# Joining and scaling the attention context ahead of its output product

## The chip, the cores and the metric

One core of a Trainium2 chip runs the whole program. The metric is the device time of one execution in microseconds; three executions of the kernel before took 811.64, 813.15 and 817.57 us.

## The reference

Four layers run one after another on 1024 rows of 256 numbers: a latent attention, a mixture of 64 experts, a recurrent mixer and a mixture of 8 experts, each added to its input and normalised. The change touches only the first. Cut to what matters:

```
kv = rmsnorm(compressed[:, :64]) @ kv_b.T         # per head: 128 of keys, 128 of values
scores = (q @ k.T) * scaling, masked to the causal half      # 16 heads
probs  = softmax(scores)
out    = concat over heads of (probs @ v)
x      = layernorm(x + out @ o_proj.T)
```

The kernel works in the latent space of 64 numbers: for a head, `context = latent.T @ exp(scores).T` has 64 rows, and the value and the output projections are multiplied once into one 64x256 matrix per head (`wvo`). The softmax's division by the row sum is made last.

## The kernel before

**Groups.** The attention goes through 8 tiles of 128 query rows; tile t looks at (t+1)*128 keys. Four heads form a group, so there are 32 groups, numbered G, four in a tile. Of each head TensorE makes scores in three passes (L1673 to L1675, high and low halves of float32) and adds the causal mask (L1760); VectorE takes the row maximum (L1133); ScalarE makes the exponential and the row sum (L868).

**Blocks.** A group's probabilities are then taken in t+1 blocks of 128 keys. For each block TensorE transposes four 128x128 pieces into one PSUM bank (L1788), ScalarE copies the rounded half out (`copy_hi`, L875), VectorE subtracts it to get the rest (`copy_lo`, L1139), and TensorE adds two products to the context in the bank `misc` (`context`, L1801 and L1803). `latent` holds high and low parts side by side, so the upper 64 and the lower 64 partitions of the context are two terms of one sum.

**Output.** When a group's context is complete, ScalarE copies it to SBUF (`copy_ctx`, L881). One group later TensorE multiplies, head by head, the context of 128 partitions with `wvo`, which holds the same 64 rows twice (`output`, L1810). VectorE scales the product of each head by the reciprocal of its row sum and adds it to the sum so far (`add_head`, L1156); the reciprocals of a group are one instruction on 128x4 numbers (`invert`, L1144).

**Order.** Each engine runs a list written out by hand: `head_slots` goes through four slots i of each G, and in a slot each engine does its part for the scores of a head of group G, for the blocks of group G-1 (at eight places, two in a slot) and for the output of group G-2. In a slot VectorE does in this order: `add_head`, steps of the normalisation and of the routing of the tile before, `copy_lo` of the first place, the row maximum, `copy_lo` of the second place, and in slot 1 `invert`. An engine does not pass an instruction that waits.

**Banks.** Blocks, outputs of heads and the small products of the routing are `tenants`: they take PSUM banks in turn, four of them while scores use short rows (the first 64 heads), then three, and seven for the last group. Before TensorE writes a bank, `take_seat` waits until the tenant before it has been read.

**Start and end.** The SP queue loads the input, the weights and a broadcast row `lnw`, in that order; a stage before the attention makes the queries, `wvo` and the keys. After the attention its last tile is normalised and routed before the experts can start.

The lines that set the order of the three engines in a slot:

```
def pe_slot(G, i, n):
    steps(G, 2 * i)
    for m in heads_at(n):
        scores(m)
    steps(G, 2 * i + 1)
    if 0 <= G - 2 < GROUPS:
        output(QUAD * (G - 2) + i)
```

Of the kernel before, what the change touches and what calls it, by code (L numbers as in the profile page):

```python
# [6 lines left out]
P = 128  # L7
# [7 lines left out]
BANK = 512  # L15
# [10 lines left out]
TWO_OUTS = SHORT - 3 * QUAD  # L26
# [12 lines left out]
def build(nc, x, xT, wq, wq_ropeT, wkv_aT, kv_ln, wkv_b, woT, router0T, gate_up0, down0, w_in, init_state,  # L39
# [5 lines left out]
    with ctx:  # L45
# [51 lines left out]
        wvo = cutA3(HEADS * HID)  # L97
# [14 lines left out]
        rinv = sb("rinv", [P, 3, QUAD])  # L112
        y = sb("y", [P, HID])
        sgd = sb("sgd", [P, 2, BANK])
        ctxT = sgd
# [127 lines left out]
        def out_of(n):  # L243

            return seat_of("out", n)[:, 0:HID]

# [4 lines left out]
        ld_x, ld_xT, ld_kv = (sem(n) for n in ("ld_x", "ld_xT", "ld_kv"))  # L251
# [8 lines left out]
        pT_ps, hi_done, lo_done, ctx_step, ctx_copied, rinv_done, out_ready, out_read = (  # L260
            sem(n) for n in ("pT_ps", "hi_done", "lo_done", "ctx_step", "ctx_copied", "rinv_done", "out_ready",
                             "out_read"))
# [158 lines left out]
        for G in range(GROUPS + 1):  # L421
            for spot in range(8):
                if route_at(G, spot):
                    tenants.append((route_at(G, spot), tile_of(G) - 1))
                tenants += [("block", b) for b in blocks_at(G - 1, spot)]
                if spot % 2 and 0 <= G - 2:
                    tenants.append(("out", QUAD * (G - 2) + spot // 2))
        tenants += [("out", QUAD * (GROUPS - 1) + i) for i in range(QUAD)]
# [6 lines left out]
        LENT = pT + [acc, half[3]] + half[0:3]  # L435
        long_rows = seat("out", TWO_OUTS)
# [52 lines left out]

        def head_slots(body):  # L490
# [5 lines left out]

        @block.sync
# [334 lines left out]
        def _(act):  # L832
            act.wait_ge(kv_ready, 1)
# [63 lines left out]
            def act_slot(G, i, n):  # L897
# [5 lines left out]
                if i == QUAD - 1 and 0 <= G - 1 < GROUPS:  # L903
                    copy_ctx(G - 1)
# [173 lines left out]
        def _(dve):  # L1078
            dve.wait_ge(ld_xT, 16)
            dve.tensor_copy(xT_hi[:], xT_in[:]).then_inc(x_split, 1)  # L1080
            dve.wait_ge(x_split, 1)
            dve.tensor_tensor(xT_lo[:], xT_in[:], xT_hi[:].bitcast(f32), ALU.subtract).then_inc(x_split, 1)
# [11 lines left out]
            def wvo_copy(m):  # L1094

                hold(dve, wvo_ps, 2 * m + 2)
                dve.tensor_copy(wvo[:, bass.ds(2 * m * HID, 2 * HID)], misc[:]).then_inc(wvo_done, 1)
# [22 lines left out]
            wvo_copy(0)  # L1120
# [4 lines left out]
            wvo_copy(1)  # L1125
            with dve.Fori(2, PAIRS) as j:
                split_weff(2 * j, 0, j)
                split_weff(2 * j + 1, 1, j)
                wvo_copy(j)
# [16 lines left out]
            def add_head(n):  # L1146

                t, h = divmod(n, HEADS)
                s, k = stat_of(n)
                dve.wait_ge(out_ready, n + 1)  # L1150
                if h == 0:
                    dve.wait_ge(ld_x, 32)
                    dve.wait_ge(rinv_done, n // QUAD + 1)
                else:
                    dve.wait_ge(out_read, n)
                dve.scalar_tensor_tensor(x1[:, t, :], out_of(n), rinv[:, s, k:k + 1], x1[:, t, :] if h else x_in[:, t, :],  # L1156
                                         ALU.mult, ALU.add).then_inc(out_read, 1)
# [18 lines left out]
            def attention_variance(t):  # L1176
                dve.wait_ge(out_read, (t + 1) * HEADS)
# [69 lines left out]
            def dve_slot(G, i, n):  # L1247
# [20 lines left out]
                go_on()  # L1268
                for b in blocks_at(G - 1, 2 * i):
# [17 lines left out]
            add_head(TILES * HEADS - 1)  # L1287
# [381 lines left out]
        def _(pe):  # L1669
# [15 lines left out]
            pe.wait_ge(ld_xT, 16)  # L1685
            pe.wait_ge(ld_kv, 16)
            for t in range(TILES):
                for c in range(HC):
# [33 lines left out]
            pe.wait_ge(x_split, 2)  # L1722
# [23 lines left out]
            def scores(n):  # L1746
# [4 lines left out]
                if n == SHORT + 1:  # L1751
                    await_read(*max((tenants[j] for j in range(long_rows) if seats[j] == 3), key=tenants.index))
# [17 lines left out]
            def await_read(before_it, k):  # L1770
                if before_it == "out":
                    pe.wait_ge(out_read, k + 1)
# [19 lines left out]
            def context(G, k):  # L1792
# [3 lines left out]
                if k == 0:  # L1796
                    if G:
                        pe.wait_ge(ctx_copied, G)
# [6 lines left out]
            def output(n):  # L1805
                G, i = divmod(n, QUAD)
                pe.wait_ge(ctx_copied, G + 1)
                take_seat("out", n)
                h = n % HEADS
                pe.matmul(out_of(n), ctxT[:, G % 2, i * P:(i + 1) * P], wvo[:, h * HID:(h + 1) * HID],  # L1810
# [356 lines left out]
```

## Time and profile before

| | us |
|---|---|
| median of 3 runs | 813.15 |
| the profiled execution | 812.66 |
| its span, first to last instruction | 810.9 |
| TensorE busy (matmuls) | 768.1 |
| VectorE busy | 555.0 |
| ScalarE busy | 397.7 |
| attention: first to last copy of a context (L881) | 80.6 to 404.2 |

### The profile page before, as it was taken

The numbers are of one execution on the slowest core, as the hardware profiler recorded it, in microseconds if no ns is written. First come the engines' busy times: TensorE is split into PE (matmuls) and PEld (weight loads), VectorE is DVE, ScalarE is ACT, GpSimd is POOL, SyncE is SP. The second block draws the span as 40 slices with busy tenths as digits, with TensorE's granted clock in tenths as the row PEclk, the third lists the DMA queues.
The fourth block names the chain that finished last, engine by engine and source line by source line (L and its number), as shares of the span: only waits on it lengthen the run. The fifth ranks groups of instructions, "written<-read, shape, count | busy, mean of one in ns | idle before, by whom it ended". The sixth has DMA issues, their size and how long they took to land.

```text
span 810.9 us, 16066 instructions
## 1 busy us (share of the span) xinstructions
PE 768.1 (95%) x4619; PEld 652.6 (80%) x4619; DVE 555.0 (68%) x1401; ACT 397.7 (49%) x899; POOL 309.7 (38%) x408
## 2 busy tenths in 40 slices
PE   8999989999999999999989999889999999999997
PEld 7887867777778788777778999788887888888885
DVE  5323778787868778777746666468858388888546
ACT  1234656656656566566514444313343266666431
POOL 2004446443433333322345665625444233333341
PEclk9999999999999999999999999999999999999999
DMA  7349971000000000009238899777651234555331
GB/s 215 100 112 340 404 296 46 29 29 28 24 26 23 21 22 22 21 15 327 87 104 296 282 363 362 267 267 278 242 184 72 72 94 153 152 152 155 111 111 52
DMA packets 61282, 120.75 MB, mean 149 GB/s; under 512 B 18016, under 2 KB 30816, under 8 KB 61088
## 3 DMA queue, kind: packets, MB, share of 16 engines
q1 hardware_dynamic: 52864, 96.59, 35.9%
q0 software_dynamic: 8352, 23.34, 8.0%
q8 instruction: 33, 0.54, 0.3%
q14 instruction: 33, 0.27, 0.1%
HBM read 76.13 MB, written 43.78 MB: 148 GB/s over the span
## 4 chain that ended last, share of the span: by engine, by line
PE 71%; DVE 10%; issue 8%; DMA 4%; POOL 3%; ACT 3%; SPq 1%; DVEq 0%; ACTq 0%; POOLq 0%
PE scores L1673 9%; PE scores L1675 9%; PE scores L1674 9%; PE scores L1897 6%; PE acc_ps L2093 5%; PE misc_ps L1803 4%; PE misc_ps L1801 4%; PE probsT_ps L1788 3%; PE probsT_ps L1810 3%; PE scores L1907 3%; PE probsT_ps L2027 3%; PE acc_ps L1788 3%; DVE xT_lo L1139 2%; DVE neg_max L1133 2%; PE probsT_ps L1886 1%
## 5 line engine op out<-in xcount | busy, mean ns | idle before, releaser
L868 ACT ACTIVATE area<-scores,neg_max 128x128 f32<-128x128 f32 (+7 forms) x128 | 94.9, 742 | 86.3 <-DVE neg_max L1133 85.9
L1133 DVE TENSOR_REDUCE neg_max<-scores 128x1 f32<-128x128 f32 (+7 forms) x128 | 95.8, 749 | 21.8 <-PE scores L1760 21.7
L711 POOL DMA_INDIRECT xe_d<-x_rows,send_i x64 | 64.0, 1001 | 55.3 <-ACT x_rows L892 38.5
L751 POOL DMA_INDIRECT ye_d<-area,home_i x64 | 61.4, 959 | 39.1 <-DVE home_i L1340 18.4
L699 POOL CAST weff_hi<-area 128x256 fp32r<-128x256 f32 x42 | 16.6, 395 | 135.1 <-PE scores L1760 87.5
L1673 PE MATMUL scores<-kT_hi,weff_hi 128*128 128x512 f32 (+3 forms) x172 | 66.6, 387 | 0.9 <-ACT area L845 0.4
L1897 PE MATMUL scores<-area 128*96 128x128 f32 x512 | 66.4, 273 | 0.4 <-issue 0.4
L1675 PE MATMUL scores<-kT_hi,weff_lo 128*128 128x512 f32 (+3 forms) x172 | 61.5, 358 | 0.0
L1674 PE MATMUL scores<-kT_lo,weff_hi 128*128 128x512 f32 (+3 forms) x172 | 61.4, 357 | 0.0
L1803 PE MATMUL misc_ps<-xT_lo,xT_hi 128*128 128x512 f32 x144 | 58.3, 405 | 1.9 <-DVE xT_lo L1139 1.8
L1897 PEld LDWEIGHTS scores<-area 128*96 128x96 f32 x512 | 59.2, 163 | 0.7 <-issue 0.6
L1788 PE MATMUL probsT_ps<-ident,area 128*128 128x128 f32 x320 | 48.1, 274 | 5.3 <-DVE xT_lo L1139 5.1
L1810 PE MATMUL probsT_ps<-area,sgd 128*128 128x256 f32 x162 | 49.6, 388 | 0.7 <-DVE xT_lo L1139 0.4
L1139 DVE TENSOR_TENSOR xT_lo<-probsT_ps,xT_hi 128x512 fp32r<-128x512 f32 x53 | 36.1, 685 | 18.3 <-ACT xT_hi L875 18.2
L1801 PE MATMUL misc_ps<-xT_hi 128*128 128x512 f32 x96 | 47.4, 494 | 0.1
L801 POOL DMA_INDIRECT area<-x_d,home x23 | 22.3, 970 | 63.7 <-ACT sgd L1013 45.3
L1673 PE MATMUL scores<-xT_hi,weff_hi 128*128 128x512 f32 x110 | 46.1, 419 | 0.0
L1788 PEld LDWEIGHTS probsT_ps<-ident,area 128*128 128x128 f32 x320 | 35.8, 142 | 11.1 <-issue 8.1
L2093 PE MATMUL acc_ps<-area 128*128 128x256 f32 x184 | 43.5, 379 | 0.8 <-DVE area L1557 0.8
L1675 PE MATMUL scores<-xT_hi,weff_lo 128*128 128x512 f32 x110 | 43.4, 394 | 0.0
L706 POOL TENSOR_TENSOR rstd<-mv,minus_half 128x1 f32<-128x1 f32 x28 | 17.0, 607 | 68.7 <-DVE mv L1165 68.7
L1674 PE MATMUL scores<-xT_lo,weff_hi 128*128 128x512 f32 x110 | 43.0, 391 | 0.0
(308 smaller groups left out, 2069.8 us busy)
## 6 DMA issues: line engine op xcount, KB each, us to landing
area<-w SPq DMA_DIRECT2D x23, 512.0 KB, 4.2
area<-gate_up SPq DMA_DIRECT2D x24, 384.0 KB, 5.1
xe_d<-area SPq DMA_DIRECT2D x8, 1088.0 KB, 11.4
ye_d<-area SPq DMA_DIRECT2D x8, 1024.0 KB, 16.9
area<-w SPq DMA_DIRECT2D x8, 1024.0 KB, 7.6
area<-ye_d SPq DMA_DIRECT2D x15, 512.0 KB, 5.0
area<-xe_d SPq DMA_DIRECT2D x28, 272.0 KB, 6.1
area<-down SPq DMA_DIRECT2D x24, 192.0 KB, 6.6
```

Source lines behind the costliest of these rows:

```text
L711: pool.indirect_dma_start(xe_d, bass.IndirectOffsetOnAxis(send_i[:, t, k:k + 1], 0), x1_rows[:, t, :], None).then_inc(sent[k % 2] if t < T ...
L868: act.activation(row_of(n)[:, 0:L], score_bank(n)[:, 0:L], ACT.Exp, bias=neg_max[:, n % 4:n % 4 + 1], accum_out=rsum[:, s, k:k + 1]).then_ ...
L1133: dve.tensor_reduce(neg_max[:, n % 4:n % 4 + 1], score_bank(n)[:, 0:(n // HEADS + 1) * P], AX.X, ALU.max, negate=True).then_inc(max_ready, 1)
L1673: pe.matmul(out_ap, lh, rh, start=start, stop=False)
L1674: pe.matmul(out_ap, lh, rl, start=False, stop=False)
L1675: return pe.matmul(out_ap, ll, rh, start=False, stop=stop)
L1788: last = pe.transpose(seat_of("block", b)[:, i * P:(i + 1) * P], row_of(QUAD * G + i)[:, k * P:(k + 1) * P], ident[:])
L1801: pe.matmul(ctx_ps[:], latent[:, k, :], pT_hi[b % 3], start=k == 0, stop=False)
L1803: pe.matmul(ctx_ps[:], latent[:, k, :], pT_lo[b % 3], start=False, stop=k == tile_of(G)).then_inc(ctx_step, 1)
L1810: pe.matmul(out_of(n), ctxT[:, G % 2, i * P:(i + 1) * P], wvo[:, h * HID:(h + 1) * HID], start=True, stop=True).then_inc(out_ready, 1)
L1897: last = pe.matmul(half[b][0:I0, part * P:(part + 1) * P], weights_of(e)[0][:, c, part * I0:(part + 1) * I0], xeT[:, b, c, :], start=c == ...
L2093: last = pe.matmul(acc[:, 0:HID], hdT[:, u, c * P:(c + 1) * P], w2_b[:, u, c, :], start=c == 0, stop=c == I1 // P - 1)
```

## The change

- ScalarE no longer copies the context as it is. It copies the upper 64 partitions of the group's first two heads to the lower 64, and the lower 64 of the other two to the upper (`cross_ctx`); VectorE adds to each the half that lay there (`join_ctx`). The result is 128x256: two heads of 64 rows on top of each other.
- The reciprocals are written out on 128x256 numbers, each one 64 times, read from a broadcast (`invert`); TensorE transposes them (`spread_scales`) and VectorE multiplies the joined context with them (`scale_ctx`).
- TensorE multiplies two heads in one contraction over 128 partitions (`output`), and sums all eight products of a tile in PSUM, in the bank `acc`. VectorE adds the input once a tile (`add_out`).
- `acc` leaves the banks in turn: three, then two, and six for the last group. A group's tenants are its blocks and one for the transposed scales.
- `wvo` holds two heads on top of each other, so its copies take 64 partitions each.
- At the start the input arrives in two halves, the second from ScalarE's queue, and so does `lnw`; VectorE splits the halves one by one.

```diff
-                banks_now = 4 if k < long_rows else 3 if k < tail else 7
+                banks_now = 3 if k < long_rows else 2 if k < tail else 6
...
-            sp.dma_start(xT_in[:], xT.rearrange("(c p) t -> p c t", p=P)).then_inc(ld_xT, 16)
+            sp.dma_start(xT_in[:, :, 0:BANK], xT_v[:, :, 0:BANK]).then_inc(ld_xT[0], 16)
...
-            sp.dma_start(lnw[:], bass.AP(kv_ln.tensor, 0, [[0, P], [1, RANK]])).then_inc(ld_head[1], 16)
...
+            act.dma_start(xT_in[:, :, BANK:], xT_v[:, :, BANK:]).then_inc(ld_xT[1], 16)
+            act.dma_start(lnw[:], bass.AP(kv_ln.tensor, 0, [[0, P], [1, RANK]])).then_inc(ld_head[1], 16)
...
-            def copy_ctx(G):
+            def cross_ctx(G):
                 act.wait_ge(ctx_step, blocks_to(G + 1))
                 if G >= 2:
-                    act.wait_ge(out_ready, QUAD * (G - 1))
-                act.copy(ctxT[:, G % 2, :], ctx_ps[:]).then_inc(ctx_copied, 1)
+                    act.wait_ge(ctx_used, scaled_at(G - 2))
+                act.copy(ctx_joined[LOW, G % 2, :], ctx_ps[HIGH, 0:HID]).then_inc(ctx_crossed, 1)
+                act.copy(ctx_joined[HIGH, G % 2, :], ctx_ps[LOW, HID:]).then_inc(ctx_crossed, 1)
...
             def invert(G):
                 dve.wait_ge(probs_ready, QUAD * (G + 1))
-                dve.reciprocal(rinv[:, G % 3, :], rsum[:, G % 3, :]).then_inc(rinv_done, 1)
...
+                wide = [P, 2, 2, RANK]
+                dve.reciprocal(rinv[:, G % 3].rearrange("p j (b r) -> p j b r", b=2),
+                               rsum[:, G % 3, :].rearrange("p (b j) -> p j b", b=2).unsqueeze(3).broadcast_to(wide)
+                               ).then_inc(rinv_done, 1)
+
+            def join_ctx(G):
+
+                dve.wait_ge(ctx_crossed, 2 * G + 2)
+                for rows, part in ((LOW, slice(0, HID)), (HIGH, slice(HID, 2 * HID))):
+                    dve.tensor_tensor(ctx_joined[rows, G % 2, :], ctx_ps[rows, part], ctx_joined[rows, G % 2, :],
+                                      ALU.add).then_inc(ctx_used, 1)
+
+            def scale_ctx(G):
+
+                dve.wait_ge(scales_and_out, scales_at(G))
+                dve.wait_ge(ctx_used, joined_at(G))
+                dve.tensor_tensor(ctxT[:, G % 2, :], seat_of("scales", G)[:, 0:HID], ctx_joined[:, G % 2, :],
+                                  ALU.mult).then_inc(ctx_used, 1)
+
+            def add_out(t):
+
+                dve.wait_ge(scales_and_out, out_at(SETS * t + SETS - 1))
+                dve.wait_ge(ld_x, 32)
+                dve.tensor_tensor(x1[:, t, :], out_ps, x_in[:, t, :], ALU.add).then_inc(ctx_used, 1)
...
-                behind = n - 1 - 2 * QUAD
-                if 0 <= behind < TILES * HEADS:
-                    add_head(behind)
+                behind = 0 <= G - 2
+                if behind and i == 0:
+                    join_ctx(G - 2)
+                if behind and i == QUAD - 1 and (G - 2) % SETS == SETS - 1:
+                    add_out(tile_of(G - 2))
...
                 go_on()
+                if behind and i == 0:
+                    scale_ctx(G - 2)
...
+            def spread_scales(G):
+
+                pe.wait_ge(rinv_done, G + 1)
+                take_seat("scales", G)
+                for j in range(2):
+                    last = pe.transpose(seat_of("scales", G)[:, j * P:(j + 1) * P],
+                                        rinv[:, G % 3, j, :], ident[:])
+                last.then_inc(scales_and_out, 1)
+
+            def output(G):
+
+                pe.wait_ge(ctx_used, scaled_at(G))
+                if G >= SETS and G % SETS == 0:
+                    pe.wait_ge(ctx_used, added_at(tile_of(G) - 1))
+                for j in range(2):
+                    m = G % SETS * 2 + j
+                    last = pe.matmul(out_ps, ctxT[:, G % 2, j * P:(j + 1) * P],
+                                     wvo[:, m * HID:(m + 1) * HID], start=m == 0, stop=m == PAIRS - 1)
+                last.then_inc(scales_and_out, 1)
...
-                if 0 <= G - 2 < GROUPS:
-                    output(QUAD * (G - 2) + i)
+                if i == 2 and 0 <= G - 2:
+                    output(G - 2)
+                if i == 3 and 0 <= G - 1 < GROUPS:
+                    spread_scales(G - 1)
```

## Rows read from the trace of the kernel before

**Rows 1.** The page, part 1: busy us, share of the span, instructions of each engine.

```profile
PE 768.1 (95%) x4619; PEld 652.6 (80%) x4619; DVE 555.0 (68%) x1401; ACT 397.7 (49%) x899; POOL 309.7 (38%) x408
```

**Rows 2.** Busy time in windows of the attention: stretch, length, engines, clock, DMA.

```profile
78.00:122.00 44.00, 40.64 (x257) 33.52 (x257) 33.51 (x98) 25.66 (x84) 20.75 (x36) 1.00 0.90 353
122.00:192.00 70.00, 67.16 (x386) 51.94 (x385) 56.47 (x137) 42.70 (x105) 34.39 (x49) 1.00 0.09 33
192.00:402.00 210.00, 200.04 (x1185) 164.49 (x1184) 162.08 (x316) 128.80 (x251) 67.32 (x93) 1.00 0.16 56
128.50:135.90 7.40, 6.83 (x43) 5.42 (x40) 6.71 (x16) 4.87 (x15) 4.91 (x7) 1.00 0.10 39
```

**Rows 3.** Chain of work that ended last, two pieces: start us, length us, what.

```profile
301.11 0.44 PE acc_ps L1788 x4
...
302.02 0.43 PE probsT_ps L1810 x2
```

**Rows 4.** Groups of VectorE's instructions by line, attention: busy us, mean ns, idle before.

```profile
L1156 DVE SCALAR_TENSOR_TENSOR x_rows<-probsT_ps,rinv,x_rows 128x256 f32<-128x256 f32 x76 | 35.8, 470 | 0.8 <-PE probsT_ps L1810 0.7
...
L1144 DVE RECIPROCAL rinv<-rsum 128x4 f32<-128x4 f32 x32 | 5.3, 166 | 0.0
```

**Rows 5.** Groups by line and shape, whole span: VectorE, 256 numbers wide; ScalarE's copies.

```profile
L1561 DVE TENSOR_TENSOR weff_lo<-misc_ps,weff_hi 128x256 fp32r<-128x256 f32 x23 | 9.8, 424 | 17.2 <-ACT weff_hi L1019 17.2
...
L881 ACT COPY sgd<-misc_ps 128x512 f32<-128x512 f32 x32 | 18.7, 583 | 12.9 <-PE misc_ps L1803 12.9
...
L1031 ACT COPY area<-acc_ps 128x256 f32<-128x256 f32 x23 | 8.6, 372 | 22.6 <-PE acc_ps L2093 22.6
```

**Rows 6.** The same view: other reciprocals, and another VectorE operation at like widths.

```profile
L1165 DVE TENSOR_SCALAR mv<-mv 128x1 f32<-128x1 f32 x28 | 4.3, 153 | 1.0
...
L1633 DVE RECIPROCAL rstd<-root 128x1 f32<-128x1 f32 x4 | 0.6, 142 | 0.0
...
L1299 DVE RECIPROCAL wsum<-wsum 128x8 f32<-128x8 f32 x1 | 0.2, 203 | 0.0
...
L1103 DVE TENSOR_SCALAR ms<-ms 128x8 f32<-128x8 f32 x1 | 0.2, 173 | 0.0
```

**Rows 7.** Waits in the attention: who for whom, us in total, times, longest.

```profile
DVE xT_lo L1139 <- ACT xT_hi L875: 36.9, 45, 1.6
...
PE probsT_ps L1788 <- DVE xT_lo L1139: 5.1, 6, 1.6
PE acc_ps L1788 <- DVE xT_lo L1139: 5.1, 6, 1.7
```

**Rows 8.** Timeline, VectorE around three reciprocals: start, length, instruction, idle before it.

```profile
120.44 0.17 DVE L1144 RECIPROCAL rinv<-rsum 128x4 f32<-128x4 f32 x1
...
120.90 0.55 DVE L1133 TENSOR_REDUCE neg_max<-scores 128x1 f32<-128x384 f32 x1
...
199.41 0.17 DVE L1144 RECIPROCAL rinv<-rsum 128x4 f32<-128x4 f32 x1
...
200.40 0.69 DVE L1139 TENSOR_TENSOR xT_lo<-acc_ps,xT_lo 128x512 fp32r<-128x512 f32 x1 [0.46 <-ACT xT_lo L875]
...
400.42 0.17 DVE L1144 RECIPROCAL rinv<-rsum 128x4 f32<-128x4 f32 x1
...
401.15 0.69 DVE L1139 TENSOR_TENSOR xT_lo<-acc_ps,xT_hi 128x512 fp32r<-128x512 f32 x1 [0.19 <-ACT xT_hi L875]
```

**Rows 9.** Timeline at the attention's end: last copy of a context, last sum.

```profile
404.23 0.59 ACT L881 COPY sgd<-misc_ps 128x512 f32<-128x512 f32 x1 [1.39 <-PE misc_ps L1803]
...
407.37 0.48 DVE L1156 SCALAR_TENSOR_TENSOR x_rows<-scores,rinv,x_rows 128x256 f32<-128x256 f32 x1
```

**Rows 10.** Timeline of the first 11 us: SP's slow issue, warming matmuls, first product.

```profile
2.30 3.77 SPq L502 DMA_DIRECT2D lnw<-kv_ln  x1
...
2.36 4.63 PE L1681 MATMUL misc_ps<-ident 128*128 128x128 f32 x20 [2.36 <-POOL ident_bf L664]
...
6.78 4.02 PE L1689 MATMUL scores<-area 128*128 128x128 f32 x32
```

More of the change, by code:

```diff
@@ L96, in build @@
         weff_lo = sb("weff_lo", [P, 2, HC, P], f32r)
-        wvo = cutA3(HEADS * HID)
+        wvo = cutA3(PAIRS * HID)
         qT = area1
@@ L111, in build @@
         rsum = sb("rsum", [P, 3, QUAD])
-        rinv = sb("rinv", [P, 3, QUAD])
+        rinv = cutA3(3, 2, P)
         y = sb("y", [P, HID])
         sgd = sb("sgd", [P, 2, BANK])
-        ctxT = sgd
+        ctx_joined, ctxT = (sgd[:, :, part * HID:(part + 1) * HID] for part in range(2))
+        LOW, HIGH = slice(0, RANK), slice(RANK, P)
         stats = sb("stats", [P, 6])
@@ L241, in build @@
         ctx_ps = misc
-        def out_of(n):
-            return seat_of("out", n)[:, 0:HID]
         half = [banks[u][:, b * BANK:(b + 1) * BANK] for u in range(2) for b in range(2)]
-        ld_x, ld_xT, ld_kv = (sem(n) for n in ("ld_x", "ld_xT", "ld_kv"))
+        ld_x, ld_kv = (sem(n) for n in ("ld_x", "ld_kv"))
+        ld_xT = [sem(f"ld_xT{b}") for b in range(2)]
         ld_head = [sem(f"ld_head{u}") for u in range(2)]
@@ L420, in build @@
         tenants = []
-        for G in range(GROUPS + 1):
+        for G in range(GROUPS + 2):
             for spot in range(8):
@@ L425, in build @@
                 tenants += [("block", b) for b in blocks_at(G - 1, spot)]
-                if spot % 2 and 0 <= G - 2:
-                    tenants.append(("out", QUAD * (G - 2) + spot // 2))
-        tenants += [("out", QUAD * (GROUPS - 1) + i) for i in range(QUAD)]
+                if spot == 7 and 0 <= G - 1 < GROUPS:
+                    tenants.append(("scales", G - 1))
         tenants += [(what, TILES - 1) for what in route_places.values()]
@@ L433, in seat @@
             return tenants.index((what, n))
-        LENT = pT + [acc, half[3]] + half[0:3]
-        long_rows = seat("out", TWO_OUTS)
+        LENT = pT + [half[3]] + half[0:3]
+        out_ps = acc[:, 0:HID]
+        long_rows = seat("scales", SHORT // QUAD - 3) + 1
         tail = seat("block", blocks_to(GROUPS - 1))
@@ L488, in stat_of, with scales_at, out_at, joined_at @@
             return n // QUAD % 3, n % QUAD
+        def scales_at(G):
+            return 2 * G + 1
+        def out_at(G):
+            return 2 * G + 2
+        def joined_at(G):
+            return 3 * G + G // SETS + 2
+        def scaled_at(G):
+            return 3 * G + G // SETS + 3
+        def added_at(t):
+            return (3 * SETS + 1) * (t + 1)
         def head_slots(body):
@@ L1078, in _ @@
         def _(dve):
[L1079 to L1082, printed above, removed]
+            x_halves = [slice(0, BANK), slice(BANK, T)]
+            for b, part in enumerate(x_halves):
+                dve.wait_ge(ld_xT[b], 16)
+                dve.tensor_copy(xT_hi[:, :, part], xT_in[:, :, part]).then_inc(x_split, 1)
+            for b, part in enumerate(x_halves):
+                dve.wait_ge(x_split, b + 1)
+                dve.tensor_tensor(xT_lo[:, :, part], xT_in[:, :, part], xT_hi[:, :, part].bitcast(f32),
+                                  ALU.subtract).then_inc(x_split, 1)
             def split_weff(h, u, i):
@@ L1124, in _ @@
             split_keys(1)
[L1125 to L1129, printed above, removed]
+            wvo_copy(1, 0, HIGH)
+            with dve.Fori(1, SETS) as s:
+                for b, rows in enumerate((LOW, HIGH)):
+                    split_weff(4 * s + 2 * b, 0, 2 * s + b)
+                    split_weff(4 * s + 2 * b + 1, 1, 2 * s + b)
+                    wvo_copy(2 * s + b, s, rows)
             def row_max(n):
@@ L1751, in scores @@
                 if n == SHORT + 1:
-                    await_read(*max((tenants[j] for j in range(long_rows) if seats[j] == 3), key=tenants.index))
+                    await_read(*max((tenants[j] for j in range(long_rows) if seats[j] == 2), key=tenants.index))
                 q = q_his[n // 2 % 3][:, n % 2, :], q_los[n // 2 % 3][:, n % 2, :]
@@ L1770, in await_read @@
             def await_read(before_it, k):
[L1771 to L1772 removed]
+                if before_it == "scales":
+                    pe.wait_ge(ctx_used, scaled_at(k))
                 elif before_it == "block":
@@ L1803, in context @@
                 pe.matmul(ctx_ps[:], latent[:, k, :], pT_lo[b % 3], start=False, stop=k == tile_of(G)).then_inc(ctx_step, 1)
[L1805 to L1810, printed above, removed]
-                          start=True, stop=True).then_inc(out_ready, 1)
+            def spread_scales(G):
[14 more added lines that the diff above has]
+                last.then_inc(scales_and_out, 1)
             def transpose_x1(t):
```

37 lines of the change are left out of this document (13 added, 24 removed).

## The prediction

> **What bounds the kernel now.** I read the page's busy times first: TensorE is busy for 95% of the span, VectorE for 68% [rows 1]. That is an average over the layers, so the windows of the attention come next, the only stage that the change reworks. TensorE is busy 92 to 96% in each of them, VectorE 76%, 81% and 77% (33.51 of 44.00, 56.47 of 70.00, 162.08 of 210.00 us), ScalarE about 60% [rows 2]. Read by that alone, TensorE is the bound and each matmul taken away is time won.
>
> The waits speak against it. VectorE's `copy_lo` waits 36.9 us for the rounded halves of one buffer from ScalarE, and TensorE's transposes wait 10.2 us, in twelve places, for `copy_lo` to free a bank [rows 7]. The three engines run in a ring: scores, maximum, exponential, rounded copy, `copy_lo`, next transposes. Where the ring is tight, a microsecond on VectorE stops TensorE. So the question for each part is what VectorE's list looks like afterwards.
>
> The Trainium skill (Perfetto Trace Analysis, Identifying the Most-Contended Engine) says that matmul busy time does not tell how near TensorE is to its limit, and that the share of weight loads tells it better. The trace agrees in direction: weight loads cover 33.52 of 44.00, 51.94 of 70.00 and 164.49 of 210.00 us [rows 2]. By busy matmuls all of the work removed below would come back as time; by weight loads a part of it was never the limit.
>
> **TensorE's part.** Before, a head's output product holds TensorE for 0.43 us [rows 3], a group's four for 1.72. After, a group has two products, 0.86, and two transposes of scales, half of the 0.44 us of four [rows 3]: 1.08 us. That is 0.64 us less in each of 32 groups, 20.5 us in all, if TensorE were never kept waiting.
>
> **ScalarE's part.** One copy of 0.583 us becomes two of 256 columns at 0.372 [rows 5]: 0.16 us more per group on an engine with 40% idle. I cost it at nothing; the exponential behind it has the row maximum to wait for anyway. Copies that cross the partitions are not in the trace; the bounds are 0, if each takes half of the one before, and 0.58 us more, if each takes all of its 0.583.
>
> **VectorE's part, the price that decides.** Removed per group: four `add_head` at 0.470 and a reciprocal at 0.166 [rows 4], 2.05 us. Added: two joins, one scaling and a quarter of `add_out`, 3.25 instructions at the 0.424 us of a 256-wide operation that reads PSUM [rows 5], 1.38 us; and a reciprocal of 128x256.
>
> No row has a reciprocal that wide. Its lower bound is any other operation of that width, 0.424 us. But reciprocals grow steeply: 142 ns for one number a partition, 166 for four, 203 for eight, while another operation goes from 153 to 173 [rows 4 to 6]. The slope is (203-142)/7 = 8.7 ns a number, three times the other's 2.9. Carried to 256, 142 + 255 x 8.7 gives 2.36 us; with the flattest pair (8.0) 2.18, with the steepest (9.25) 2.50. I take 2.3, since the rows of the same operation are nearer than those of other ones.
>
> The Trainium skill (VectorE: DVE Perf Modes, First, the fixed hardware budget) says that the reciprocal is an iterative division with a repeat count of 8. By that rule the sum is the one below; by the 256-wide row VectorE would have a little less to do than before, and the second rival would hold.
>
> So VectorE gets 1.38 + 2.3 - 2.05 = 1.63 us more per group.
>
> **Where that falls.** The wide reciprocal stands where the small one stood, at the end of slot 1, and ahead of the next `copy_lo` or maximum.
>
> Tiles 0 to 3: in tile 1 the next maximum follows the reciprocal within 0.3 us, after one `add_head` and with no idle time [rows 8]; there VectorE is nearly the bound. In the densest stretch it reached 6.71 of 7.40 us, 90% [rows 2], so I let it be at most that busy. The first window needs (33.51 + 8 x 1.63)/0.90 = 51.7 us instead of 44, 7.7 more; the second (56.47 + 13.0)/0.90 = 77.2 instead of 70, 7.2 more.
>
> Tiles 4 to 7: sixteen groups. Here `copy_lo` comes next and starts 0.56 to 1.43 us after the reciprocal's end, 1.08 in the mean (the first, 0.82, and the last, 0.56, are shown [rows 8]): room left by the vanished `add_head` and the wait for ScalarE. The reciprocal grows by 2.13 us, so `copy_lo` comes 1.05 us later, and behind it the bank that TensorE's next transposes need, or the block that the next product needs. In sixteen groups that is 16.8 us. The 0.64 us that TensorE saves lies ahead of these waits and mostly lengthens them. The joins and the scaling, 1.27 us in slot 0, lie beside ScalarE's exponential and rounded copy, which `copy_lo` waits for; I cost them at nothing; without that cover they would be 0.8 us per group more than the `add_head` they replace.
>
> **Banks.** With two in turn a block waits for the one two before it, whose `copy_lo` its context product awaits right after. The second block of each group instead takes the bank of the scales and so waits for `scale_ctx`. In tiles 6 and 7 only 0.22 + 0.44 us of TensorE's work lie between the last context product and that block, against 2 x 0.372 + 3 x 0.424 = 2.02 us of crossing, joining and scaling: a wait of some 1.4 us in 8 groups, 11 us. I take nothing, as ScalarE cannot copy this block before the last head's exponential and the first block are through; 11 stays as the upper bound.
>
> **Start and end.** SP's issue of `lnw` took 3.77 us and leaves its queue. But the warming matmuls ran from 2.36 to 6.99, and the first product with the input, on which all that follows waits, started among their last at 6.78 [rows 10]: 0, between 1 us won by earlier weights and 1 lost to two queues loading at once. The half-partition copies of `wvo` do as many columns as before: 0. At the end 3.62 us lay between the last copy's start and the last sum's end [rows 9]; afterwards it is 0.74 + 1.27 + 0.86 + 0.42 = 3.3 and two more hand-overs, 0.3 more.
>
> **Sum.** 7.7 + 7.2 + 16.8 + 0.3 = 32 us on the profiled 812.66, which lies 0.49 under the median: **845 us**.
>
> **Rivals.**
> 1. TensorE is the bound all through, and the reciprocal is no longer than other operations: 20.5 us come back, 792 us. For it speaks the 95%; against it the waits and the slope of three reciprocals. It decides wherever VectorE keeps idle time behind the reciprocal. Chance 0.08.
> 2. The reciprocal is short, but the wait for the scales' bank in tiles 6 and 7 (11 us) and the ring eat most of what TensorE saves: 812.66 - 20.5 + 11 = 803 to 813, say 810. Chance 0.08.
> 3. Nothing of VectorE's extra work is hidden: 32 x 1.63 = 52 us, with the bank's 11 on top 864 to 876. Against it speak 77% of VectorE busy in tiles 4 to 7. Chance 0.06.
>
> That leaves 0.78 for the forecast. Its own range runs from 819, with VectorE 95% busy in the early tiles (4.9 + 3.2 - the start's 1) and little lost later, to 864. To hold 8 in 10 I go from 817 to 867.
>
> A measurement of this kernel can tell about 1%, 8 us, from no change. Faster than 805: rival 1 and a small part of rival 2, 0.09. Within: the rest of rival 2 and the forecast's low edge, 0.10. Slower than 821: 0.81.
>
> **What would show it.** Right: 32 reciprocals of 128x256 at 2.2 to 2.5 us each; VectorE's busy time in the attention up by some 50 us while TensorE's falls; TensorE's waits for `copy_lo` after slot 1 grown by about 1 us a group; the attention some 30 us longer, all else unchanged. Wrong: a wide reciprocal near 0.4 us would bring down the whole forecast; a long one with the attention not longer would mean that VectorE's idle time lies where I saw none.

## The result, and the profile after

The change made the kernel slower: 868.76 us in the median (867.21 to 869.99) against 813.28 for the kernel before beside it, a ratio of 1.068 with a 95% interval of 1.064 to 1.073. The prediction had the direction; 845 us was 24 us too low, and the time lies just over the end of the range, 867.

The page of the changed kernel, busy time by engine; it answers to [rows 1]:

```profile
PE 773.3 (89%) x4555; PEld 652.4 (75%) x4555; DVE 596.4 (69%) x1379; ACT 405.3 (47%) x931; POOL 309.3 (36%) x408
```

TensorE went from 95% to 89%, VectorE from 68% to 69%, and the span grew by 57 us. So the added time is mostly waiting. VectorE has 41 us more to do, and TensorE is busy for 5 us more, although the change was to take 20.5 us off it: it ran at a lower clock, as the windows show.

The windows of the attention, laid over the same tiles as [rows 2] (tiles 0 and 1, 2 and 3, 4 to 7): start and end, length, busy time of PE, PEld, DVE, ACT and POOL, TensorE's granted clock, DMA share, GB/s:

```profile
80.00:136.00 56.00, 40.63 (x241) 32.37 (x242) 42.96 (x92) 27.79 (x90) 20.99 (x35) 0.97 0.69 271
136.00:218.00 82.00, 65.67 (x372) 49.76 (x371) 66.53 (x131) 44.37 (x114) 33.31 (x49) 0.98 0.08 28
218.00:460.00 242.00, 205.50 (x1150) 166.27 (x1149) 184.34 (x306) 132.86 (x266) 67.85 (x94) 0.94 0.14 49
```

The three stretches grew by 12, 12 and 32 us. All of the loss is in the attention. The granted clock, 1.00 in each stretch before, is 0.94 to 0.98. Of the prediction's signs of being right, VectorE's 50 us more came as 42 (252.06 to 293.83 over the three stretches); TensorE's fall did not come (307.84 to 311.80).

VectorE's new groups in the attention: busy time and mean, then idle before. The first answers to the 128x4 reciprocal of [rows 4], the others to the 256-wide operation of [rows 5]:

```profile
L1167 DVE RECIPROCAL area<-rsum 128x256 f32<-128x256 f32 x32 | 55.8, 1743 | 0.0
L1175 DVE TENSOR_TENSOR sgd<-misc_ps,sgd 64x256 f32<-64x256 f32 x62 | 26.2, 422 | 14.4 <-ACT sgd L897 13.0
L1182 DVE TENSOR_TENSOR sgd<-probsT_ps,sgd 128x256 f32<-128x256 f32 x27 | 11.4, 421 | 2.1 <-DVE sgd L1175 0.5
```

The reciprocal takes 1.74 us, not 2.3. Joins and scaling took the 0.42 us forecast for them.

TensorE's waits in the attention; they answer to [rows 7] (in total, times, longest):

```profile
PE probsT_ps L1824 <- DVE sgd L1182: 32.1, 21, 2.6
PE probsT_ps L1824 <- DVE xT_lo L1161: 10.0, 11, 1.9
PE misc_ps L1839 <- DVE xT_lo L1161: 6.9, 15, 1.4
```

The transposes' wait for `copy_lo` did not grow (10.2 us before). That of the context products did; before, it was

```profile
PE misc_ps L1803 <- DVE xT_lo L1139: 1.8, 5, 0.7
```

A new wait stands above both: transposes that wait for `scale_ctx` to free the bank of the scales. With two more of them that write to a bank of another name (3.4 us) it comes 23 times, 35.5 us in all. This is the wait that the prediction saw and took nothing for. The timeline of TensorE shows one of them (start, length, instruction, idle time before it):

```profile
414.06 0.60 PE L1824 MATMUL probsT_ps<-ident,area 128*128 128x128 f32 x4
417.29 0.63 PE L1824 MATMUL probsT_ps<-ident,area 128*128 128x128 f32 x4 [2.63 <-DVE sgd L1182]
417.67 0.68 PE L1708 MATMUL scores<-kT_hi,weff_hi 128*128 128x512 f32 x1
```

And the stretch right behind it, in the windows (columns as above):

```profile
417.84:421.24 3.40, 3.40 (x13) 2.50 (x13) 1.27 (x2) 0.60 (x1) 2.66 (x3) 0.51 1.03 334
```

TensorE idles for 2.63 us and then runs at 0.51, the 1.2 GHz level: this wait is paid twice. The attention has 11 stretches of 3.41 us at that level, 37.5 us in all; the profiled execution of the kernel before had none there.

### The profile page after: what moved, and what is told of

It reads as the page before. It is cut to its first block, busy times and chain, and to the rows that moved or that the text cites. A ratio compares the mean times of both kernels' runs of the same rounds, so it can differ in the third digit from the quotient of the medians.

```text
span 868.2 us, 15777 instructions
## 1 busy us (share of the span) xinstructions
PE 773.3 (89%) x4555; PEld 652.4 (75%) x4555; DVE 596.4 (69%) x1379; ACT 405.3 (47%) x931; POOL 309.3 (36%) x408
## 4 chain that ended last, share of the span: by engine, by line
PE 61%; DVE 19%; issue 10%; ACT 5%; POOL 3%; DMA 2%; DVEq 0%; SPq 0%; ACTq 0%; POOLq 0%
PE scores L1708 8%; PE scores L1710 8%; PE scores L1709 8%; PE scores L1947 6%; PE probsT_ps L1824 5%; PE acc_ps L2143 5%; DVE xT_lo L1161 4%; DVE area L1167 3%; PE scores L1957 3%; DVE neg_max L1155 3%; PE misc_ps L1839 3%; PE misc_ps L1837 3%; DVE sgd L1175 2%; PE probsT_ps L2077 2%; PE acc_ps L1857 2%
## 5 line engine op out<-in xcount | busy, mean ns | idle before, releaser
L1824 PE MATMUL probsT_ps<-ident,area 128*128 128x128 f32 x508 | 83.0, 291 | 42.5 <-DVE sgd L1182 32.1
L1155 DVE TENSOR_REDUCE neg_max<-scores 128x1 f32<-128x128 f32 (+7 forms) x128 | 94.7, 747 | 31.7 <-PE scores L1796 31.6
L1824 PEld LDWEIGHTS probsT_ps<-ident,area 128*128 128x128 f32 x508 | 60.8, 151 | 53.5 <-issue 30.5
L712 POOL CAST weff_hi<-area 128x256 fp32r<-128x256 f32 x42 | 16.6, 394 | 158.4 <-PE scores L1796 110.7
L1161 DVE TENSOR_TENSOR xT_lo<-probsT_ps,xT_hi 128x512 fp32r<-128x512 f32 x85 | 57.8, 682 | 18.4 <-ACT xT_hi L890 17.9
L890 ACT ACTIVATE xT_hi<-probsT_ps 128x512 fp32r<-128x512 f32 x85 | 50.1, 594 | 37.9 <-PE probsT_ps L1824 37.9
L1839 PE MATMUL misc_ps<-xT_lo,xT_hi 128*128 128x512 f32 x144 | 60.1, 417 | 6.9 <-DVE xT_lo L1161 6.9
L1167 DVE RECIPROCAL area<-rsum 128x256 f32<-128x256 f32 x32 | 55.8, 1743 | 0.0
```

Source lines behind the costliest of these rows:

```text
L1155: dve.tensor_reduce(neg_max[:, n % 4:n % 4 + 1], score_bank(n)[:, 0:(n // HEADS + 1) * P], AX.X, ALU.max, negate=True).then_inc(max_ready, 1)
L1161: dve.tensor_tensor(pT_lo[b % 3], seat_of("block", b)[:], pT_hi[b % 3].bitcast(f32), ALU.subtract).then_inc(lo_done, 1)
L1167: dve.reciprocal(rinv[:, G % 3].rearrange("p j (b r) -> p j b r", b=2), rsum[:, G % 3, :].rearrange("p (b j) -> p j b", b=2).unsqueeze(3). ...
L1824: last = pe.transpose(seat_of("block", b)[:, i * P:(i + 1) * P], row_of(QUAD * G + i)[:, k * P:(k + 1) * P], ident[:])
L1839: pe.matmul(ctx_ps[:], latent[:, k, :], pT_lo[b % 3], start=False, stop=k == tile_of(G)).then_inc(ctx_step, 1)
```

## The experiments

**Theories.** They have the letters of the expectations. A: the one wait for the scales' bank costs the time. B: the wide reciprocal on VectorE costs it. C: the clock is a cause of its own. D: one bank less in turn costs it. And T (rival 1's root): TensorE's time is what counts, so the 20.5 us saved must be in the sum. The time of each tile, from the last context copy of a tile to that of the next, tells where a run lost.

**The scales later, the reciprocal narrow, and both.** `late` moves the transposes of the scales and their seat to the slot where they are used:

```diff
-                if spot == 7 and 0 <= G - 1 < GROUPS:
-                    tenants.append(("scales", G - 1))
+                if spot == 1 and 0 <= G - 2 < GROUPS:
+                    tenants.append(("scales", G - 2))
...
-                if behind and i == 0:
+                if behind and i == 1:
                     scale_ctx(G - 2)
...
-                if i == 3 and 0 <= G - 1 < GROUPS:
-                    spread_scales(G - 1)
+                if i == 0 and 0 <= G - 2 < GROUPS:
+                    spread_scales(G - 2)
```

`narrow` inverts four numbers, and GpSimd writes them out:

```diff
+                    pool.tensor_copy(rinv[:, (G - 1) % 3].rearrange("p j (b r) -> p j b r", b=2),
+                                     rinv_n[:, (G - 1) % 3, :].rearrange("p (b j) -> p j b", b=2).unsqueeze(3)
+                                     .broadcast_to([P, 2, 2, RANK])).then_inc(rinv_done, 1)
...
-                wide = [P, 2, 2, RANK]
-                dve.reciprocal(rinv[:, G % 3].rearrange("p j (b r) -> p j b r", b=2),
-                               rsum[:, G % 3, :].rearrange("p (b j) -> p j b", b=2).unsqueeze(3).broadcast_to(wide)
-                               ).then_inc(rinv_done, 1)
+                dve.reciprocal(rinv_n[:, G % 3, :], rsum[:, G % 3, :]).then_inc(root_done, 1)
```

> The changed kernel, but the transposed scales of a group are made one slot later (after the first two places of the next G) and scaled into the context at once, so that no block waits for a bank that holds scales. Theory A, the bank of the scales (TensorE waited 35.5 us for scale_ctx in the changed kernel): 35 us of waits go, and with them most of the stretches at the halved clock: 825 to 838 us. Theory B, the reciprocal of 1.74 us in VectorE's list: nothing changes in that list but the place of one 0.42 us operation: 860 to 869 us. Theory C, the clock, as a cause of its own: the half-clock stretches stay at 14, the time falls by at most the 35 us.

> The changed kernel, but VectorE inverts 128x4 numbers as before (0.17 us) and GpSimd writes them out 64 times each (its 256-wide copies took 0.39 us). VectorE's list is 1.58 us shorter in each of 32 groups. Theory B: most of it comes back, 825 to 840 us. Theory A: the wait for scale_ctx hangs on crossing, joining and scaling, not on the reciprocal: 35 us of it stay, and the time is 852 to 862 us.

> Late scales and the narrow reciprocal together. If A and B are the two causes and the clock only follows them: no loss is left and a part of TensorE's saved 20.5 us shows: 795 to 810 us, faster than before, with at most three stretches at the halved clock. If something else holds the time (ScalarE's crossing, one bank fewer): 815 us or more.

`late` took 871.7 us (ratio to the kernel before 1.070, 1.065 to 1.076), `narrow` 845.5 (1.038, 1.032 to 1.043), `both` 850.2 (1.045, 1.039 to 1.051). So B holds for 23 us, and A falls in this form: the wait was moved, not taken away. `both`, forecast at 795 to 810 us if A and B were all, shows that a third cause is left. TensorE's waits in the attention of `late`:

```profile
PE probsT_ps L1824 <- DVE xT_lo L1161: 32.9, 30, 2.1
PE probsT_ps L1846 <- DVE xT_lo L1161: 11.2, 9, 1.6
```

The wait for `scale_ctx` is gone from the head of the list, and the same transposes wait as long for `copy_lo` (32.1 for the one in the changed kernel, 32.9 for the other now), the transposes of the scales with them. The kernel's list of tenants tells why. In `late` the scales, or a small product of the routing, often stand between two blocks of a group. With two banks the second of these takes the bank of the block right before it, and must wait until that one has been copied out. Of the blocks of groups 14 to 30, where two banks are in turn, 22 stand so; all 22 wait, 23.4 us in all. The 51 that follow the block two before wait in seven places, 6.9 us. With two banks, whoever is pushed out of one place waits in the next.

**Each suspect alone, in the kernel before.** `wide_before` has only the reciprocal of 128x256; `onefewer_before` only one bank less in turn:

```diff
-                dve.reciprocal(rinv[:, G % 3, :], rsum[:, G % 3, :]).then_inc(rinv_done, 1)
+                dve.reciprocal(rinv[:, G % 3], rsum[:, G % 3, :].unsqueeze(2).broadcast_to([P, QUAD, RANK])
+                               ).then_inc(rinv_done, 1)
```

```diff
-        LENT = pT + [acc, half[3]] + half[0:3]
+        LENT = pT + [half[3]] + half[0:3]
...
-                banks_now = 4 if k < long_rows else 3 if k < tail else 7
+                banks_now = 3 if k < long_rows else 2 if k < tail else 6
```

> The kernel before with one edit: the reciprocal is written out 64 times each on VectorE, as in the change; add_head reads one of the 64. VectorE's list is 1.58 us longer per group, banks and products are as before. Theory B: the first two windows by VectorE at 90% busy +7 and +7, the last sixteen groups 16 x (1.58 - 1.08) = 8: 835 us. Theory A: VectorE had the room, under 821 us.

> The kernel before with one edit: the bank acc leaves the turn (3 banks, then 2, then 6), as in the change; it stays unused in the attention. Theory D, one bank fewer: late scales and narrow reciprocals together still lost 35 us, all in tiles 3 to 7, where TensorE waited 31 us for copy_lo; so two banks alone cost the kernel before about as much: 838 to 860 us, the loss in tiles 3 to 7 and none in tiles 0 to 2. Rival, joining and crossing on the way to the bank of the context: this kernel has neither and stays under 821 us.

The reciprocal alone gave 840.8 us (1.032, 1.026 to 1.039), the banks alone 851.9 (1.049, 1.044 to 1.054). VectorE's timeline in `wide_before`, tile 1:

```profile
132.42 1.74 DVE L1144 RECIPROCAL area<-rsum 128x256 f32<-128x256 f32 x1
134.07 0.39 DVE L1157 SCALAR_TENSOR_TENSOR x_rows<-probsT_ps,area,x_rows 128x256 f32<-128x256 f32 x1
134.38 0.55 DVE L1133 TENSOR_REDUCE neg_max<-scores 128x1 f32<-128x384 f32 x1
```

The maximum behind the reciprocal starts without idle time: the whole of it is in the way. Now the banks, in the timeline of `onefewer_before`, with both engines:

```profile
301.74 0.69 DVE L1139 TENSOR_TENSOR xT_lo<-probsT_ps,xT_hi 128x512 fp32r<-128x512 f32 x1 [1.52 <-ACT xT_hi L875]
...
302.35 1.08 DVE L1133 TENSOR_REDUCE neg_max<-scores 128x1 f32<-128x896 f32 x1
...
302.58 0.67 PE L1810 MATMUL probsT_ps<-area,sgd 128*128 128x256 f32 x2 [0.76 <-ACT xT_hi L875]
303.35 0.68 DVE L1139 TENSOR_TENSOR xT_lo<-probsT_ps,xT_hi 128x512 fp32r<-128x512 f32 x1
...
304.18 0.30 PE L1788 MATMUL probsT_ps<-ident,area 128*128 128x128 f32 x1 [0.93 <-DVE xT_lo L1139]
```

TensorE's transposes at 304.18 need the bank that `copy_lo` reads until 304.03, and that `copy_lo` stands in VectorE's list behind a maximum of 1.08 us. Neither a reciprocal nor a scale is in the chain. What stands between the two blocks is an output product (302.58): it takes the other bank, so the next block takes that of its direct predecessor. This holds for 29 blocks of groups 14 to 30, and 28 of them wait, 22.4 us; with three banks, in the kernel before, for 17, of which five wait, 6.7 us. The loss here, 40 us, is larger than in the changed kernel; four outputs a group share the two banks here.

**The bank given back.** `turn` puts `acc` back among the banks (4, 3 and 7) and lets the two products of a group be summed in a bank in turn, which VectorE adds once a group; `turn_narrow` has the narrow reciprocal as well.

```diff
+                if spot == 5 and 0 <= G - 2 < GROUPS:
+                    tenants.append(("out", G - 2))
...
-                    last = pe.matmul(out_ps, ctxT[:, G % 2, j * P:(j + 1) * P],
-                                     wvo[:, m * HID:(m + 1) * HID], start=m == 0, stop=m == PAIRS - 1)
+                    last = pe.matmul(seat_of("out", G)[:, 0:HID], ctxT[:, G % 2, j * P:(j + 1) * P],
+                                     wvo[:, m * HID:(m + 1) * HID], start=j == 0, stop=j == 1)
```

> The changed kernel with one part undone: acc is back in the turn (4, 3, 7 banks); the two products of a group are summed in a bank of the turn, and VectorE adds them to the row once a group (0.42 us more in three groups of four). Theory D: tiles 3 to 7 lose no more than the wide reciprocal costs there, 825 to 842 us. Rival, the bank of the scales or the joins: 858 to 875 us.

> The same with the narrow reciprocal, written out by GpSimd. Theory D with the reciprocal: no loss is left, and of TensorE's 20.5 us a part comes back: 797 to 812 us. Rival: 838 us or more.

`turn` took 840.1 us (1.032, 1.027 to 1.038), `turn_narrow` 814.2 (1.001, 0.999 to 1.004). The 797 to 812 us forecast for it, with a part of TensorE's 20.5 us back, did not come. With these the two suspects make a square (medians, us):

| | wide reciprocal | narrow reciprocal |
|---|---|---|
| two banks (three, early) | 868.8 | 845.5 |
| three banks (four, early) | 840.1 | 814.2 |

The reciprocal costs 23 to 26 us, the bank 29 to 31, and the one hardly changes the other's price. (The row of three banks also has VectorE's sum once a group in place of once a tile, so the bank alone may be worth a little more.) TensorE's waits for `scale_ctx` in `narrow` and in `turn_narrow`, which keep the scales in the early place:

```profile
PE probsT_ps L1827 <- DVE sgd L1185: 30.8, 21, 2.6
PE probsT_ps L1833 <- DVE sgd L1186: 10.6, 13, 1.6
```

This wait falls by 20 us with the third bank; the two kernels lie 31 us apart. By tiles, from the time of each tile in the profiled runs: the narrow reciprocal gives back 16.8 of the 18.5 us lost in tiles 0 to 2, and two banks (`both` against the kernel before) cost 34.7 us in tiles 3 to 7 and nothing ahead of them, where three were left.

**The clock.** `fill` is the changed kernel with ten spare products ahead of the first two blocks' transposes in tiles 6 and 7, where the wait for the scales stands:

```diff
+                at = seat_before("block", b)
+                if at is not None and tenants[at][0] == "scales" and tile_of(G) >= 6 and k <= 1 and G + 1 < GROUPS:
+                    m = QUAD * (G + 1) + 2
+                    pe.wait_ge(probs_ready, heads_before(m))
+                    run_idle(10, score_bank(m))
```

> The changed kernel, but in tiles 6 and 7 TensorE makes ten spare products of 128 columns (about 1.1 us at the full clock) where it waits for scale_ctx; their bank is written anew right after. Theory C, the halved clock costs time of its own (products of 512 columns went from 0.40 to 0.63 us in such a stretch): some five of the 14 stretches go, 858 to 864 us. If the clock only shows that TensorE waits: 867 to 873 us.

862.0 us (1.061, 1.056 to 1.066), 6 to 7 us less with more work. The stretches at the 1.2 GHz level in the attention fell from 11 to 5, and their time from 37.5 to 20.5 us; the span's mean granted clock rose from 0.974 to 0.984. In tiles 6 and 7 themselves all five went, and these tiles got 6.4 us shorter, 1.3 us for each. So the slow clock is a cost of its own, on top of the wait (C). As it goes where the banks come back, I take it for a part of what the square gives to the two causes, not for a third beside them; no run separates it there.

**The start.** `start_before` is the kernel before with only the input in halves and `lnw` on ScalarE's queue, as in the change's diff.

> The kernel before with the new start alone: the input in two halves, the second and lnw from ScalarE's queue, split half by half. The forecast's step: 0, between -1 and +1 us, 811 to 814 us. Rival: all kernels with this start began their first exponential at 73.8 to 74.5 us of the span, those without at 73.3 to 73.9, so it costs 0.5 to 1 us; then 812 to 814. A gain of over 1 us would speak against both.

812.7 us (0.999, 0.997 to 1.001). SP's slow issue did not go away with `lnw`. SP's issues in the changed kernel, where [rows 10] had 3.77 us on `lnw`:

```profile
2.30 4.74 SPq L522 DMA_DIRECT2D area<-wq  x1
```

The next DMA in the queue has it, at the same time and longer.

**The best version.** `turn_late` is `turn_narrow` with the later scales; `turn_late_oldstart` has the old start as well.

> Banks in turn restored, the narrow reciprocal, and the scales spread late and used at once: of the 10.6 us that TensorE still waited for scale_ctx with scales in the early place, most goes. If these waits are on the path: 802 to 809 us, faster than before. If the ring of maximum, exponential, rounded copy and copy_lo sets the pace and TensorE's own work does not: 811 to 816 us.

> The same with the start of the kernel before. If the new start costs 0.5 to 1 us, this one is that much faster than its neighbour: 801 to 808 us by the waits, 810 to 815 us by the ring.

811.5 us (0.997, 0.995 to 0.999) and 812.6 (0.999, 0.997 to 1.001). With the bank there, the later scales cost nothing. The best version is 0.1 to 0.3% ahead of the kernel before, though it has all of the saving that was to take 20.5 us off TensorE. Its windows, over the very stretches of [rows 2]:

```profile
78.00:122.00 44.00, 38.37 (x247) 30.35 (x247) 32.75 (x98) 27.63 (x92) 22.55 (x42) 1.00 0.90 355
122.00:192.00 70.00, 63.11 (x366) 47.48 (x364) 54.83 (x136) 44.07 (x112) 39.86 (x59) 1.00 0.09 33
192.00:402.00 210.00, 196.45 (x1170) 159.83 (x1168) 163.49 (x322) 131.55 (x268) 73.44 (x109) 1.00 0.16 56
```

TensorE is 10 us less busy in these 324 us (14 over the whole span, 753.9 against 768.1), and so idle for 10 us longer.

**Is TensorE's time worth anything?** `refill` and `refill3` put six and three spare products a group ahead of the output products of `turn_late`; `narrow_out_before` is the kernel before with 160 of the 256 columns of each output product computed and the others left out; `spare_before` adds three spare products to that kernel.

```diff
                 take_seat("out", G)
+                run_idle(6, seat_of("out", G))
```

```diff
-                pe.matmul(out_of(n), ctxT[:, G % 2, i * P:(i + 1) * P], wvo[:, h * HID:(h + 1) * HID],
+                kept = 160
+                pe.matmul(out_of(n)[:, 0:kept], ctxT[:, G % 2, i * P:(i + 1) * P], wvo[:, h * HID:h * HID + kept],
```

> The kernel turn_late with TensorE's saved work put back: six spare products of 128 columns before the output products of each group, in the bank that these then write. 32 x 6 x 0.108 us = 20.7 us more of TensorE's work, about the 20.5 us that the change takes away. If the ring sets the pace and TensorE has that room: 811 to 817 us, within 1% of turn_late. If TensorE is the bound in the attention: 826 to 833 us.

> The version with three banks, the narrow reciprocal and the later scales (811.5 us), with three spare products per group ahead of the output products. One spare product is two records of about 0.11 us each, so three are 0.65 us a group and 20.8 us over the 32 groups: the time that the change takes off TensorE, put back. If TensorE had that room all along (the ring of scores, maximum, exponential, transposes and copies sets the pace), 811 to 817 us. If TensorE sets the pace, all of it comes back: 826 to 833. If the loss is in proportion to the run with six (33 of 43 us lost), about 827; if about 10 us are hidden in any case and the rest counts in full, about 822.

> The kernel before, and only TensorE gets less to do: each output product computes 160 of its 256 columns (the other 96 are left out; VectorE adds the same 256 numbers, whatever stands there). By the measured 0.43 us for 256 columns that is 0.16 us less a product and 20.5 us over 128 products, just what the change was to take off TensorE, with no new wait, reciprocal or bank. If that time is worth nothing, as the prediction held, 810 to 815 us. If TensorE sets the pace throughout, 792. If it is worth what refill3 lost by putting it back (13 of 20.8 us), about 800.

> The kernel before with three spare products per group on TensorE, in one piece ahead of the third head's output product: 0.65 us a group, 20.8 us over 32 groups, as in refill3. Taking 20.5 us away from this kernel gave 2.5 us. If TensorE has room in its ring in both directions, 811 to 817 us. If the kernel stands at the edge, so that less work buys nothing and more costs in full, 828 to 834. If one piece of this length in this place costs what it cost in refill3 (13 us), 822 to 828.

In `refill` I put in twice what I meant: the chain of work shows its six products as 1.34 us, so 42.9 us in all.

```profile
309.04 1.34 PE probsT_ps L1723 x12
```

It took 844.3 us (1.040, 1.037 to 1.043). `refill3` took 824.6 (1.015, 1.011 to 1.018), `narrow_out_before` 809.6 (0.997, 0.995 to 0.999), `spare_before` 826.9 (1.018, 1.015 to 1.022). The chain of `narrow_out_before` has each product at 0.27 us, where [rows 3] had 0.43:

```profile
295.96 0.27 PE probsT_ps L1811 x2
```

Taken off by itself, 20.5 us of TensorE's work is worth 0.3%, 2.5 us, the same as the best version won. A part of the rest went into the clock: the median of the granted clock over its 12 executions is 0.991, over the 17 of the kernel before beside it 0.995. The profiled one shows where, in the first window of [rows 2]:

```profile
78.00:122.00 44.00, 40.36 (x255) 35.47 (x254) 30.85 (x92) 24.86 (x80) 19.04 (x33) 0.88 0.91 357
```

Its tiles 0 and 1 took 2.2 us longer than in the profiled execution before; tiles 2 to 7, at a clock of 1.00, took 4.6 us less. So even at the full clock only 4.6 of the 15.4 us taken off in those tiles come back.

Put in, 20.8 us cost 13 us by the medians (14 and 15 by the ratios), both in the version with less work and in the kernel with more. So it is not TensorE's total that counts, or `refill3` and `spare_before`, which differ by the 20.5 us, would not lie 2 us apart. The step from three spare products to six, 22.1 us more, cost 19.7. So the ring hides some 7 to 10 us of added work, and beyond that work counts nearly in full; less work than before is worth little. Whether the place counts too, one piece against four shaves of 0.16 us, no run tells: none adds the work in four places. Which step of the ring takes the shaved time back is not shown either, beyond the clock's part.

## Why the prediction was wrong, by its steps

**Mechanism, right in the main.** The ring of engines sets the pace and not TensorE's total: `narrow_out_before` bears it out, and rival 1, that 20.5 us come back, falls. The reciprocal is long, and its place in VectorE's list makes its length count.

**The step that failed: the banks.** "I take nothing" stood for a cost of 29 to 31 us, nearly three times its upper bound of 11. The argument had two halves. The first, that a block which waits for "the one two before it, whose `copy_lo` its context product awaits right after" loses nothing, was right: put beside the kernel's list of tenants, the changed kernel's trace has 62 such blocks in groups 14 to 30, and they wait in six places, 2.0 us in all. The second half failed. A block that takes the bank of the scales waits in all 17 cases, 27.9 us, 1.6 us each. (The 17 that follow their direct predecessor wait in five places, 8.0 us.) The prediction saw this wait in the eight groups of tiles 6 and 7 alone, at 1.4 us. Of the 23 waits of the whole attention, seven lie in these tiles, 14.9 us, and 16 in tiles 2 to 5, 20.5 us, where it saw none. And it let the wait be covered, since ScalarE could not copy the block earlier anyway. But TensorE does not pass the waiting transposes: in the rows above, the scores behind them start at 417.67, after the 2.63 us of idle time, and the next maximum, exponential and copies need these scores. That this holding up of the scores is what makes the wait count is my reading of the rows; that most of the wait goes when the bank comes back is shown by `turn_narrow`. `late` shows that a better place for the scales does not help while only two banks are in turn: then other blocks follow their direct predecessor.

**The reciprocal, right in sum, wrong in its parts.** 31.7 us were forecast, 23 to 26 came.
- Tiles 4 to 7: 1.05 us a group after 1.08 of slack, 16.8 us. With the measured length the same step gives 1.743 - 0.166 - 1.08 = 0.50 us, 8.0 in 16 groups; the wide reciprocal costs 7.7 there (changed kernel against `narrow`) and 7.1 (`turn` against `turn_narrow`). The step was right, and the size of one term wrong.
- Tiles 0 to 3: 14.9 us, from the rule that VectorE may be 90% busy. Measured are 17.9 (changed kernel against `narrow`) and 16.6 (`turn` against `turn_narrow`), but with a shorter reciprocal, for which the rule would have given 5. VectorE is busy 77% and 81% in the first two windows after, so it never came near 90. The place in the list decided, not the share: in tiles 0 to 2 some 1.4 of the 1.58 us of growth went through in each of 12 groups.

**Costed at nothing, and so it was.** ScalarE's crossings took 0.37 and 0.36 us as forecast; the groups of its copies in the attention:

```profile
L896 ACT COPY sgd<-misc_ps 64x256 f32<-64x256 f32 x32 | 11.8, 370 | 16.5 <-PE misc_ps L1839 16.0
L897 ACT COPY sgd<-misc_ps 64x256 f32<-64x256 f32 x31 | 11.3, 364 | 0.8
```

`turn_narrow` holds the crossings, joins, scaling and half-partition copies together, and ties with the kernel before, so they cost no more than the little that TensorE's saving is worth. The start is nothing by `start_before`. At the end the last group's crossing starts at 461.92 and the last sum ends at 465.76, 3.84 us against 3.62 [rows 9], 0.2 more where 0.3 was forecast:

```profile
461.92 0.37 ACT L896 COPY sgd<-misc_ps 64x256 f32<-64x256 f32 x1 [2.68 <-PE misc_ps L1839]
...
465.34 0.42 DVE L1189 TENSOR_TENSOR x_rows<-acc_ps,area 128x256 f32<-128x256 f32 x1 [1.22 <-PE acc_ps L1857]
```

**Left out.** The granted clock was in no term. It fell most in the kernels with the waits for the bank and the reciprocal, and a little in `narrow_out_before`, which has neither; the 6 to 7 us of `fill` are what a run shows of its cost.

**The rivals.** Rival 3's 864 to 876 held the time, for another reason than its own: not all of VectorE's work was laid bare (23 to 26 us of its 52), and the bank cost three times its 11. Rival 2 falls too: `narrow` has its short reciprocal and its two banks, and took 845.5 us, not 803 to 813. One half of it is right: in `turn_narrow`, with the bank given back, the ring eats all of what TensorE saves, 814 us.

## What to carry to other kernels

Count the buffers in turn against the whole list of who takes them, and write out for each whom it follows. Two banks were enough for blocks that follow the block two before; one more tenant in each group was not covered, and wherever it was put some block waited 1.1 to 1.6 us. When a wait on one engine is called covered by another engine's work, look at what stands behind the wait in its own list. An engine at 95% busy in a ring gave 0.3% for 20 us of its work; test such a saving by taking columns off a product before building the layout that saves it.

## What the runs showed that I had not expected

- A reciprocal costs 142 ns for one number a partition, 166 for 4, 203 for 8 [rows 4, 6] and 1743 for 256: the slope at few numbers, 8 to 9 ns, overstates the wide one, 6.3.
- After an idle time of 2.63 us TensorE ran 3.4 us at the 1.2 GHz level, and the chain has a 512-column product at 0.43 us there. Spare work in such waits made the kernel 6 to 7 us faster, 1.3 us for each slow stretch that went.
- SP's slow issue belongs to a place in its queue, or to a time, more than to a DMA: at 2.30 us it was 3.77 us on `lnw` before, 4.74 on the weights' DMA that took its place.
- 20.8 us more work at one place on TensorE costs the same 13 us in a kernel that has 20.5 us less of it, and the next 22.1 us cost 19.7.
